# The first loads and the first products of a fused two-layer kernel, put in another order

## What is computed

```python
def lora_add(base, inp, A, B):           # RANK 16, SCALE 0.5
    Ab = A[layer_idx][lora_indices]; Bb = B[layer_idx][lora_indices]
    t = jnp.einsum('bri,bni->bnr', Ab, inp)
    return base + jnp.einsum('bor,bnr->bno', Bb, t) * SCALE
gate = lora_add(jnp.einsum('bnh,fh->bnf', x, W_gate), x, A_gate, B_gate)
up   = lora_add(jnp.einsum('bnh,fh->bnf', x, W_up), x, A_up, B_up)
act  = jax.nn.silu(gate) * up            # F = 1376 features
down = lora_add(jnp.einsum('bnf,hf->bnh', act, W_down), act, A_down, B_down)
x = x + ffn0(down)                       # W0, bias and eight mixed adapters
x = x + ffn1(cond1(x))                   # masked linear layer, then 64 experts, top 16
```

## Time and profile before

| | us |
|---|---|
| median of three runs | 355.14 |
| lowest, highest | 354.69, 355.90 |
| the profiled execution, its own time | 355.97 |
| its span, first to last instruction | 354.2 |
| outside the span | 1.77 |
| TensorE matmul busy | 350.0 (99%) |
| VectorE, ScalarE, GpSimd busy | 200.3, 143.9, 79.1 |
| HBM read, written | 34.97 MB, 2.10 MB |

### The profile page before, as it was taken

One profiled execution on the slowest core, in us unless ns is written; L12 is line 12 of the kernel. 1 busy time (PEld: TensorE's weight loads), 2 busy tenths in 40 slices (PEclk: granted clock), 3 DMA queues, 4 the chain that ended last, 5 costly groups with the idle time before them and its releaser, 6 DMA issues.

```text
span 354.2 us, 4621 instructions
## 1 busy us (share of the span) xinstructions
PE 350.0 (99%) x1682; PEld 294.7 (83%) x1682; DVE 200.3 (57%) x302; ACT 143.9 (41%) x196; POOL 79.1 (22%) x86
## 2 busy tenths in 40 slices
PE   8999999999999999999999999999999999999997
PEld 8799888888888888888888898888888888888885
DVE  4678765245523452676583575869888867501102
ACT  5467644323432343455463561566352443201100
POOL 1452657864440003000000000000041145002200
PEclk9999999999999999999999999999999999999999
DMA  6934333332130043498219009110051021201011
GB/s 220 316 102 155 104 112 109 117 93 81 34 104 0 0 159 117 109 365 318 59 30 287 26 10 407 58 40 23 0 179 60 0 61 60 59 31 59 30 61 59
DMA packets 14802, 37.31 MB, mean 105 GB/s; under 512 B 2272, under 2 KB 4224, under 8 KB 13504
## 3 DMA queue, kind: packets, MB, share of 16 engines
q1 hardware_dynamic: 11920, 31.18, 25.6%
q0 software_dynamic: 2432, 5.57, 5.7%
q10 hardware_dynamic: 432, 0.33, 0.3%
HBM read 34.97 MB, written 2.10 MB: 105 GB/s over the span
## 4 chain that ended last, share of the span: by engine, by line
PE 99%; issue 0%; DVE 0%
PE ps L1157 29%; PE ps L1159 29%; PE ps L1158 29%; PE ps L1179 3%; PE ps L1309 3%; PE ps L1399 1%; PE ps L1386 1%; PE ps L1194 1%; PE ps L1187 1%; PE ps L1198 1%; PE ps L1202 1%; PE ps L1234 1%; PE ps L1408 0%; PE ps L1417 0%; DVE x L1149 0%
## 5 line engine op out<-in xcount | busy, mean ns | idle before, releaser
L1157 PE MATMUL ps<-x_hl,w_hl 128*128 128x512 f32 x144 | 56.1, 390 | 0.0
L1158 PE MATMUL ps<-x_hl,w_hl 128*128 128x512 f32 x144 | 56.1, 390 | 0.0
L1159 PE MATMUL ps<-x_hl,w_hl 128*128 128x512 f32 x144 | 56.0, 389 | 0.0
L462 POOL TENSOR_TENSOR am_hl<-am_raw,am_hl 128x512 fp32r<-128x512 f32 x8 | 11.0, 1389 | 137.8 <-ACT am_hl L479 137.8
L418 POOL DMA_INDIRECT b_raw<-b_gu,row_of x32 | 32.1, 1002 | 27.7 <-DVE b_st L780 19.6
L800 DVE TENSOR_TENSOR glu<-glu,ps 128x512 f32<-128x512 f32 (+1 forms) x22 | 14.9, 683 | 38.8 <-PE ps L1179 26.2
L1159 PEld LDWEIGHTS ps<-x_hl,w_hl 128*128 128x128 f32 x144 | 27.0, 188 | 5.7
L1157 PEld LDWEIGHTS ps<-x_hl,w_hl 128*128 128x128 f32 x144 | 27.1, 188 | 5.3
L511 ACT ACTIVATE glu<-ps 128x512 f32<-128x512 f32 (+1 forms) x22 | 12.8, 588 | 45.9 <-PE ps L1179 45.0
L1158 PEld LDWEIGHTS ps<-x_hl,w_hl 128*128 128x128 f32 x144 | 27.1, 188 | 5.2
L1157 PE MATMUL ps<-act,wd_hl 128*128 128x512 f32 x80 | 31.1, 389 | 0.0
(11 more groups left out here) (151 smaller groups left out, 728.6 us busy)
## 6 DMA issues: line engine op xcount, KB each, us to landing
wc_raw<-mask_w SPq DMA_DIRECT2D x8, 1024.0 KB, 7.1
w_raw<-w_gu SPq DMA_DIRECT2D x8, 512.0 KB
wd_raw<-w_dn SPq DMA_DIRECT2D x10, 256.0 KB
w_raw<-w_t SPq DMA_DIRECT2D x2, 1024.0 KB, 7.3
x<-x_t SPq DMA_DIRECT2D x2, 1024.0 KB, 6.2
am_raw<-a_moe SPq DMA_DIRECT2D x8, 256.0 KB, 2.7
bm_raw<-b_moe SPq DMA_DIRECT2D x4, 512.0 KB, 3.7
x_raw<-x_t SPq DMA_DIRECT2D x7, 256.0 KB, 7.1
```

What stands on the lines that cost most here:

```text
L462: nc.gpsimd.tensor_tensor(am_hl[:, j % AM_SLOTS, 1], am_raw[:, j % 2], am_hl[:, j % AM_SLOTS, 0].bitcast(F32), ALU.subtract).then_inc(am_l ...
L1157: nc.tensor.matmul(out, w_high, m_high, start=start, stop=False)
L1158: nc.tensor.matmul(out, w_high, m_low, start=False, stop=False)
L1159: return nc.tensor.matmul(out, w_low, m_high, start=False, stop=stop)
```

## The change

It moves loads between queues and products in their order, and splits one load in two. W's slice 0 of tile 0 is loaded by ACT as two loads of 64 KB, the gate half and then the up half, each with a semaphore. Slice 0 of tile 1's chunk goes from SP's queue to ACT's, behind them. The index table goes from ACT's queue to SP's, where five loads stand ahead of it. DVE makes high and low part of the gate half as soon as it is there; ACT makes the high part of the up half, DVE its low part. TensorE takes the three products of the gate half first, then those of the up half. The number of products is the same.

```diff
--- before.py
+++ after.py
@@ -191,6 +191,7 @@
         dma_const, dma_small = sem("dma_const"), sem("dma_small")
         dma_w_first = [[sem(f"dma_w_first{u}_{c}") for c in range(3)] for u in range(2)]
         w0_used = sem("w0_used")
+        dma_up_first, gate_first_hi, gate_first_lo = sem("dma_up_first"), sem("gate_first_hi"), sem("gate_first_lo")
         row_step = sem("row_step")
         warm_set = sem("warm_set")
         dma_x0 = [None] + [sem(f"dma_x0_{k}") for k in range(1, KD)]
@@ -275,10 +276,10 @@
             for h in range(2):
                 sp.dma_start(x_raw[:, 0, h * PAIR:h * PAIR + PAIR],
                              x_t[:, 0, h * PAIR:h * PAIR + PAIR]).then_inc(dma_x0_pair[h], 16)
-            sp.dma_start(w_raw[1][:, 0], w_gu[1, :, 0]).then_inc(dma_w_first[1][0], 16)
             load_x0(1)
             for u in range(2):
                 sp.dma_start(w_raw[u][:, 1], w_gu[u, :, 1]).then_inc(dma_w_first[u][1], 16)
+            sp.dma_start(small_sb[:], small_in).then_inc(dma_small, 16)
             for u in range(2):
                 load_x0(2 + u)
                 sp.dma_start(w_raw[u][:, 2:KD], w_gu[u, :, 2:KD]).then_inc(dma_w_first[u][2], 16)
@@ -529,8 +530,9 @@
                     silu(2 * f + 2 + s, s, 4 * (1 - u) + 2 * s)
                     act_high(2 * f + 2 + s, s, f, s)
 
-            act_e.dma_start(w_raw[0][:, 0], w_gu[0, :, 0]).then_inc(dma_w_first[0][0], 16)
-            act_e.dma_start(small_sb[:], small_in).then_inc(dma_small, 16)
+            act_e.dma_start(w_raw[0][:, 0, 0], w_gu[0, :, 0, 0]).then_inc(dma_w_first[0][0], 16)
+            act_e.dma_start(w_raw[0][:, 0, 1], w_gu[0, :, 0, 1]).then_inc(dma_up_first, 16)
+            act_e.dma_start(w_raw[1][:, 0], w_gu[1, :, 0]).then_inc(dma_w_first[1][0], 16)
             act_e.wait_ge(warm_set, 1)
             nc.scalar.activation(warm[:, 1:2], warm[:, 0:1], ACT.Silu)
 
@@ -542,7 +544,9 @@
                 pair = slice(h * PAIR, h * PAIR + PAIR)
                 act_e.wait_ge(dma_x0_pair[h], 16)
                 copy(x_hl[:, 0, 0, pair], x_raw[:, 0, pair]).then_inc(x_hi if h else x_pair_hi, 1)
-            act_e.wait_ge(w_hi, 1)
+                if h == 0:
+                    act_e.wait_ge(dma_up_first, 16)
+                    copy(w_hl[0][:, 0, 0, 1], w_raw[0][:, 0, 1]).then_inc(w_hi, 1)
             w_first_high(1, slice(0, 1), 0)
             x_high(1, 0)
             for u in range(2):
@@ -824,12 +828,17 @@
                 low(w_hl[u][:, 1, ks], w_raw[u][:, ks], w_hl[u][:, 0, ks]).then_inc(w_lo, 1)
 
             dve.wait_ge(dma_w_first[0][0], 16)
-            nc.vector.tensor_copy(w_hl[0][:, 0, 0:1], w_raw[0][:, 0:1]).then_inc(w_hi, 1)
+            nc.vector.tensor_copy(w_hl[0][:, 0, 0, 0], w_raw[0][:, 0, 0]).then_inc(gate_first_hi, 1)
+            dve.wait_ge(gate_first_hi, 1)
+            low(w_hl[0][:, 1, 0, 0], w_raw[0][:, 0, 0], w_hl[0][:, 0, 0, 0]).then_inc(gate_first_lo, 1)
             for h in range(2):
                 pair = slice(h * PAIR, h * PAIR + PAIR)
                 dve.wait_ge(x_hi if h else x_pair_hi, 1)
                 low(x_hl[:, 1, 0, pair], x_raw[:, 0, pair], x_hl[:, 0, 0, pair]).then_inc(x_lo if h else x_pair_lo, 1)
-                w_first_low(h, slice(0, 1), h + 1)
+                if h == 0:
+                    dve.wait_ge(w_hi, 1)
+                    low(w_hl[0][:, 1, 0, 1], w_raw[0][:, 0, 1], w_hl[0][:, 0, 0, 1]).then_inc(w_lo, 1)
+            w_first_low(1, slice(0, 1), 2)
             x_low(1, 0)
             for u in range(2):
                 w_first_low(u, slice(1, 2), 3 + u)
@@ -1226,24 +1235,32 @@
                     else:
                         adapt(b_st[1] if f else b_other, FIRST_BANK[n] + m, s)
 
-            def project_pair(h):
+            def pair_of(h, m, part_w, part_x):
                 pair = slice(h * PAIR, h * PAIR + PAIR)
-
-                def pass_of(part_w, part_x):
-                    for m in range(2):
-                        nc.tensor.matmul(ps[:, FIRST_BANK[0] + m, pair], w_hl[0][:, part_w, 0, m], x_hl[:, part_x, 0, pair],
-                                         start=h == part_w == part_x == 0, stop=False)
-
-                pe.wait_ge(w_hi, 1)
-                pe.wait_ge(x_hi if h else x_pair_hi, 1)
-                pass_of(0, 0)
-                pe.wait_ge(x_lo if h else x_pair_lo, 1)
-                pass_of(0, 1)
-                pe.wait_ge(w_lo, 1)
-                pass_of(1, 0)
-
-            for h in range(2):
-                project_pair(h)
+                nc.tensor.matmul(ps[:, FIRST_BANK[0] + m, pair], w_hl[0][:, part_w, 0, m], x_hl[:, part_x, 0, pair],
+                                 start=h == part_w == part_x == 0, stop=False)
+
+            def first_pair(m):
+                pe.wait_ge(w_hi if m else gate_first_hi, 1)
+                pe.wait_ge(x_pair_hi, 1)
+                pair_of(0, m, 0, 0)
+                pe.wait_ge(w_lo if m else gate_first_lo, 1)
+                pair_of(0, m, 1, 0)
+                pe.wait_ge(x_pair_lo, 1)
+                pair_of(0, m, 0, 1)
+
+            def second_pair():
+                pe.wait_ge(x_hi, 1)
+                for m in range(2):
+                    pair_of(1, m, 0, 0)
+                    pair_of(1, m, 1, 0)
+                pe.wait_ge(x_lo, 1)
+                for m in range(2):
+                    pair_of(1, m, 0, 1)
+
+            for m in range(2):
+                first_pair(m)
+            second_pair()
             project_first(1, 0)
             for k in range(1, KD):
                 for u in range(2):
```

## The result

The changed kernel takes 356.17 us (median of 22 runs, 355.38 to 358.08), the kernel before in the same comparison 355.00 (22 runs, 354.41 to 356.57): ratio 1.0034, interval [1.0024, 1.0044]. It is slower, by about 1.2 us, just beyond the 1.07 us that I had called the least that can be told from no change; the interval reaches to both sides of that. My 355.2 was too low; 356.17 lies inside the range of 353.8 to 356.4, and "slower" had got a chance of 0.16. Three of the 22 runs took 357.79 to 358.08, all at a mean granted clock of 0.995, where the other 19 had 0.999 or 1.000 and a median of 355.94.

A forecast was written before the change was run, and what follows sets the result against it. TensorE was taken as the bound for 99% of the span, with savings only in its early waits. The later of b_first's and x's shifts moved the end +0.05: 355.97 to 356.02, less 0.83 to the median, 355.2; range 353.8 to 356.4.

The forecast's parts named there:

- three signs of being wrong: Adapter products beginning before 27.6 or after 29.2, the table landing near 5 us, or a new wait after 30 us.
- The first products: TensorE's start and first twelve products, with tile 1's slice 0 on ACT's queue: -0.1 us, from -0.3 to +0.2.
- Each wait swallows what was won ahead of it: TensorE's waits at 12.89, 17.03 and 28.43 stand in a row; time won earlier is lost at the next.
- the saving that I called possible: At most the sum of TensorE's last three waits, 1.69 us, and a few tenths in the first products.
- The wait at 12.89: TensorE's 1.17 us wait for tile 1's slices 2 and 3: -0.3 us, between 0 and -1.17.
- The first rival: Transfers at the start get faster and all three later waits shrink: -1.2 us, 353.9 us; chance 0.22.
- x's second halves: SP's later x loads, issued 1.2 us later: landing shift 0, up to 1.2 later or 1 us forward.
- The index table: Issued sixth on SP's queue at 3.2, landing at about 7.2, 2.0 us later, delaying POOL's and SP's adapter loads.
- b_first comes too late: Rival: its second gather lands after 20.95 and delays t_st and the end: +1.27 us, or 356.4; chance 0.14.
- The third rival: Early products begin no earlier, as ACT's third issue and table load delay x piece 0: 355.2, counted within the forecast's 0.64.

The follow-up runs named there:

- the reordered kernel before: Kernel before with one edit: DVE makes the low part t_st ahead of the last tile's fourth low part; 355.16 us, ratio 1.0007.
- The second profile of before: Profile from a repeat comparison of the kernel before, with no edit; median 355.31 us, ratio 1.0005, profiled execution 356.29 us.
- the shorter chain: Kernel before with the index table seventh on SP's queue and t_st made ahead of the last tile's fourth low part on DVE; 355.65 us, ratio 1.0014.

## Why the prediction was off

The measured time lies in my range, but that was luck. It is outside the forecast's own range of 354.4 to 356.0, and the upper end of 356.4 stood there for b_first, which came in time. None of my three signs of being wrong appeared either, with the adapter products at 28.23; none of them looked at the first 8 us, where the loss arose.

**The first products: here the step failed.** I wrote that tile 1's slice 0 "comes on ACT's queue, issued at about 1.8, when SP issued it before", and took -0.1 for the whole part, +0.2 at worst. The issue time was right (1.78), the landing wasn't. In SP's queue the slice had only the two x pieces ahead of it, and the x slice behind it; on ACT's it lands with that x slice, 5.3 us after its issue instead of 4.1. I had put this term at nothing but issue times. Measured alone, it is +1.2 us by the medians, six times my upper end. The rule that I had put beside this term (loads from several engines interleave on the same 16 DMA engines) says that nothing is won by the move. I read it as "so nothing changes". What the one queue had given, and two don't, is the order. The Trainium skill has the rest of it (DMA: Bandwidth & Descriptors, section "Queues, rings and completion order"): each DMA engine goes round robin over the queues that have work. The landings agree: 5.1 us for SP's 256 KB and 5.3 for the slice beside it, 3.9 us for SP's 128 KB and 4.2 for the slice beside that.

**"Each wait swallows what was won ahead of it": true of the profile, not of the kernel.** In the two profiled executions it holds to the tenth. By the rows of the matmuls, which start a little behind their weight loads, tile 0's slice 1 begins at 7.90 before and at 9.07 after, 1.17 us late, and the adapter products at 28.46 and 28.45: the later waits had cost before as much as the delay costs after. That is less than the 1.69 us that I had summed from the idle times of the weight loads (the 1.17 before 12.89 is 0.75 in the matmuls' rows), so the saving that I called possible was too large by half a us. But the kernel's median was 1.0 us below the profiled execution, so in most of its runs those later waits can't have been there at that length, and could swallow little. I had seen the 0.83 and treated it as an offset to subtract at the end. It was most likely the very wait that I let absorb the cost.

**The wait at 12.89.** I took -0.3 out of 0 to -1.17; it went wholly (ACT's copy at 10.37), although the load was issued at 5.36 and not at 5.09, since the issue ahead of it took 0.70 us instead of 0.43. In the reordered kernel before, with the load at 5.09 and the table on ACT, that copy is at 10.57, so the wait can go without the change. The first rival was right that it goes, and nothing shows its reason. In the run with the table in eleventh place POOL issued no transfer before 13.74, and still tile 1's slices 2 and 3 came late: this row of its DMA view, from an issue at 5.10, gives a landing at 12.0.

```profile
w_raw<-w_gu SPq DMA_DIRECT2D x1, 256.0 KB, 6.9
```

So this landing was late without any transfer of POOL's. The Trainium skill's best guess for its slower engines, the one cited beside the first rival (DMA: Bandwidth & Descriptors, section "Latency and other measured facts"), doesn't explain it in this run.

**x's second halves.** I gave them a shift of 0, and 1 us forward at most. They landed 4.0 us after their issue (median), not 10.1, and ACT copied all four from 14.72 on, where before the last was copied at 20.41. The second profile of before had 9.9 us and the wait at 13.37, the reordered one 5.4 us and no such wait. The long landings of these loads and of tile 1's slices came together in both profiles of before.

**The index table.** Issue and delay: predicted 3.2 and 7.2, issued 3.19 and landed 4.6 us later, at 7.8; POOL 2.6 to 3.0 us late instead of 2.0. a_raw did cost ACT 0.85 us of waiting, but TensorE came there later still. b_first landed early enough: its second gather began at 14.70 and was read at 19.65, 4.9 us later rather than the 7.5 of before, as I had thought possible. The rival "b_first comes too late" had the right size of the end result (356.4) and the wrong place. Alone the table's move costs 0.75 us (there in seventh place); under the delay at 7.57 it is hidden, since the changed kernel loses 1.2 and not 2.0.

**The third rival** (first products no earlier) came true: first product at 4.18, x piece 0's copy at 3.67.

**The chances** don't add up as I wrote them. 0.22 less 0.02 plus 0.02 is 0.22 for faster, not 0.20, and with 0.16 for slower 0.62 is left for the same.

**What stays open:** why the table in sixth or seventh place costs 0.75 us. Four profiles with table and tile 1's slice both on SP have a wait of 0.4 to 1.6 us near 12.7, but so have the two of before. A rival that no run takes apart is the place itself: in seventh place the table pushes the load of tile 1's slices 2 and 3 back from 5.09 to 5.56 or 5.57 on SP's queue, and ACT copies them at 11.92, 12.06 and 12.29 in the three such profiles, against 10.57 in the reordered kernel before. With the table in eleventh place the load was issued at 5.10 and came late all the same. The slow early products (2.63 and 2.56 us in the two runs with the table in seventh place and no split) aren't it alone, since with the split they took 1.85 us and the time was 355.70. It is not the chain to t_st (the shorter chain gave nothing), and the wait for a_raw shows only when the table is later still. Also open is what makes the late landings late.

## What to carry to other kernels

In this kernel moving a load to another engine's queue gave it company, not speed: it landed with what stood beside it in the other queue, so what is needed first is better left first in one queue. Before letting a wait absorb a cost, compare the profiled execution's own time with the median: if it is as much above it as the wait is long, the wait is probably not there in most runs.

## What the runs showed that I had not expected

TensorE's early products run at the pace of the 1.2 GHz level (0.21 us for 256 columns) and later ones at that of 2.4 GHz (0.12), with the granted clock column at 1.00 throughout, and the change comes at a different time from profile to profile although the zero products before it are the same. Twelve weight loads of slice 0, first in the kernel with w ahead of x's slice 3 (all at the slow pace), then in the one with the table in eleventh place (fast from about the fourth on):

```profile
4.21 2.64 PEld L1235 LDWEIGHTS ps<-x_hl,w_hl 128*128 128x128 f32 x12 [0.28 <-DVE w_hl L828]
```
```profile
4.22 1.75 PEld L1234 LDWEIGHTS ps<-x_hl,w_hl 128*128 128x128 f32 x12 [0.29 <-DVE w_hl L827]
```

That is 0.9 us, nearly as much as this change is about. The clock record of the traces themselves fits: it begins only with the full level, at 7.02 us in the first of these two and at 4.49 in the second (5.72 in the profile of before, 4.28 to 7.02 over the eleven profiles that have such a record). Ahead of it the column shows 1.00 without a record behind it. Neither edit touches these products; but each kernel has one profile only, and the two of the unchanged kernel before differ by 0.18 (2.26 and 2.08), so how much of the 0.9 is chance isn't shown. In the changed kernel a difference of this kind is hidden as long as the twelve end before 7.57, when tile 1's slice comes. The first of the two kernels reached the adapter products at 27.54 without any wait, later than the 27.17 of the reordered kernel before with its wait of 0.28.
